# Mask and maximum matmuls on half the rows each, with new orders of work, in a two-layer decoder kernel

## The reference

```
x += window_attention(norm(x))          # layer 0: 16 heads, 7 neighbours, weights times a learned profile
x += masked_attention(norm(x), ctx)     # q = norm(x), k = v = ctx, 16 heads of 16; keys where mask == 0 get -1e9
x += slot_mixer(norm(x))                # top 8 of 64 slots, softmax, one GRU step, back by the same weights
x += causal_attention(norm(x))          # layer 1: causal, bias by position
x += cross_attention(norm(x), ctx)      # k, v from ctx, no mask
x += quantized_mlp(norm(x))             # ternary weights, hidden 1024, 3-tap conv, silu
```

## Time and profile before

| | us |
|---|---|
| median of 3 runs (3355.11 to 3357.54) | 3356.95 |
| the profiled execution | 3370.52 |
| its span, first to last instruction | 3368.7 |

### The profile page before, as it was taken

How to read it: one execution, slowest core, us unless ns; L and a number is a source line. 1 busy time by engine, 2 the same in 40 slices (tenths; PEclk the granted TensorE clock), 3 DMA queues, 4 the chain that set the end, 5 groups by cost and what they waited for, 6 DMA issues and landing times.

```text
span 3368.7 us, 61751 instructions
## 1 busy us (share of the span) xinstructions
PE 2962.4 (88%) x23406; PEld 2084.8 (62%) x23406; DVE 2265.4 (67%) x6662; ACT 2286.4 (68%) x5005; POOL 730.6 (22%) x1360
## 2 busy tenths in 40 slices
PE   4798978999889999899988999889998999989985
PEld 3566755666656666566665666556665666656663
DVE  6744499546885469854787548864589546985476
ACT  2358764788657786577765787657865778657783
POOL 1420023310332012320133102321032301232000
PEclk8899998999999999999999999999999999999997
DMA  4000000000000000000000000000000000000000
GB/s 153 1 1 1 1 26 12 9 1 4 23 20 1 1 15 12 20 1 1 15 23 9 1 4 15 20 9 1 4 23 20 1 1 15 12 20 1 1 5 10
DMA packets 43483, 43.59 MB, mean 13 GB/s; under 512 B 8577, under 2 KB 41185, under 8 KB 43185
## 3 DMA queue, kind: packets, MB, share of 16 engines
q1 hardware_dynamic: 41200, 36.46, 3.7%
q10 hardware_dynamic: 1984, 3.18, 0.3%
HBM read 31.24 MB, written 8.39 MB: 12 GB/s over the span
## 4 chain that ended last, share of the span: by engine, by line
PE 55%; DVE 20%; ACT 18%; issue 3%; POOL 2%; DMA 1%; SPq 0%; DVEq 0%; ACTq 0%; POOLq 0%
PE banks L1186 10%; PE banks L1219 9%; PE banks L1265 6%; PE banks L1228 4%; PE banks L1327 3%; ACT chain_arena L1025 3%; DVE chain_m L704 3%; PE banks L1261 3%; PE banks L1204 3%; ACT chain_arena L1046 2%; DVE chain_arena L898 2%; PE banks L1291 2%; ACT chain_xn L973 2%; DVE chain_arena L738 2%; PE banks L1411 2%
## 5 line engine op out<-in xcount | busy, mean ns | idle before, releaser
L1219 PE MATMUL banks<-chain_arena 64*128 64x256 f32 x3072 | 441.3, 410 | 18.3 <-DVE chain_m L704 15.5
L704 DVE TENSOR_REDUCE chain_m<-banks 128x4 f32<-128x512 f32 x512 | 330.7, 684 | 164.7 <-PE banks L1219 163.7
L1046 ACT ACTIVATE chain_arena<-chain_arena,chain_m 128x128 f32<-128x128 f32 x1024 | 322.9, 393 | 76.1 <-DVE chain_m L697 75.5
L1219 PEld LDWEIGHTS banks<-chain_arena 64*128 64x128 f32 x3072 | 278.6, 192 | 146.5 <-issue 84.7
L697 DVE CUSTOM_DVE_ANT_0 chain_arena<-banks,pos_bias 128x128 f32<-128x128 f32 x1024 | 226.5, 286 | 142.5 <-PE banks L1219 141.9
L1525 POOL TENSOR_SCALAR chain_rv<-chain_sq 128x2 f32<-128x2 f32 x160 | 35.2, 220 | 1263.8 <-ACT chain_xn L973 1262.0
L1265 PE MATMUL banks<-chain_arena 64*128 64x256 f32 x2048 | 293.0, 405 | 0.0
L1265 PEld LDWEIGHTS banks<-chain_arena 64*128 64x128 f32 x2048 | 177.4, 187 | 120.7 <-issue 109.0
L980 ACT ACTIVATE chain_xn<-chain_xa,chain_nm,chain_rs 128x256 f32<-128x256 f32 x384 | 207.5, 593 | 64.3 <-POOL chain_nm L1529 64.0
L671 DVE CUSTOM_DVE_ANT_0 chain_xa<-banks,chain_xa 128x256 f32<-128x256 f32 x320 | 122.4, 420 | 181.2 <-PE banks L1327 171.4
L1579 POOL TENSOR_TENSOR chain_arena<-chain_arena 128x512 f32<-128x512 f32 x128 | 165.4, 1304 | 279.7 <-DVE chain_arena L782 279.1
(11 more groups left out here) (315 smaller groups left out, 6894.9 us busy)
## 6 DMA issues: line engine op xcount, KB each, us to landing
chain_xn<-in_ctx SPq DMA_DIRECT2D x32, 256.0 KB, 2.8
chain_xa<-in_x SPq DMA_DIRECT2D x32, 256.0 KB, 3.1
out<-chain_xa SPq DMA_DIRECT2D x32, 256.0 KB, 2.2
chain_arena<-in_mask SPq DMA_DIRECT2D x32, 128.0 KB, 3.7
f_w1t<-in_w1t ACTq DMA_DIRECT2D x1, 1024.0 KB, 7.1
f_w2t<-in_w2t ACTq DMA_DIRECT2D x1, 1024.0 KB, 14.4
wqkv0T<-in_wqkv0T ACTq DMA_DIRECT2D x1, 768.0 KB, 16.8
whh<-in_whh SPq DMA_DIRECT2D x1, 768.0 KB, 10.0
```

The source lines that it names most:

```text
L704: e.tensor_reduce(m, s.rearrange("p (j o) t -> p j o t", o=2), AX.X, ALU.max, negate=True).then_inc(*done(f"{tag}_mx{u}"))
L1046: ex = e.activation(s, s, ACT.Exp, scale=-1.0, bias=max_of(t["m"], u // GROUPS, row_group(u), a))
L1219: mm[i] = e.matmul(c.ps[:, i, 2 * T * j:2 * T * j + 2 * T], t["qh"][p, j, x, b, :], flat(t["kx"][p, j, b]), start=not masked, stop=not mas ...
```

## The change

Three things. The key mask's matmul is split by rows as the scores are: for bank i it reads rows 64 i to 64 i + 63 of `first` and of the mask, and `first` has a row of ones at row 0 and at row 64. The matmul that spreads the maxima does the same with `pick` and mT; the three rows it needs lie in its half already. And all five lists of ORDER are replaced by others of the same length, with each chain as often in them as before. What is computed stays the same.

```diff
     if masked:
         for i in range(2):
-            e.matmul(c.ps[:, i, :], k["first"][:], spread(t["mask_bf"][:, T * b:T * b + T], 1, PER), start=True, stop=False)
+            p = slice(64 * i, 64 * i + 64)
+            e.matmul(c.ps[:, i, :], k["first"][p], spread(t["mask_bf"][p, T * b:T * b + T], 1, PER), start=True, stop=False)
...
         for i in range(2):
-            e.matmul(ps[:, i, :], k["pick"][:, 2 * i + o, :], flat(t["mT"][:, b]), start=True, stop=False)
+            p = slice(64 * i, 64 * i + 64)
+            e.matmul(ps[:, i, :], k["pick"][p, 2 * i + o, :], flat(t["mT"][p, b]), start=True, stop=False)
...
-        "rows_of": np.stack([(p // 32 == i) & (p % 32 < 3) for i in range(GROUPS)] + [p == 0], 1).astype(f),
+        "rows_of": np.stack([(p // 32 == i) & (p % 32 < 3) for i in range(GROUPS)] + [p % 64 == 0], 1).astype(f),
```

The lists, cut to the first and the last line of three of them:

```diff
     "sync": (
-        "0011223301031232001133220011332200113322001133220011332200113322"),
+        "0011223313123020131320201133220011332200113322001133220011332200"),
     "pool": (
-        "0132001133220132000101331313021232201232013201320132010310031123300201101122000033301111031101332203"
+        "1320113322001321011133311232202300321020302103210320131321133021112201333111310011333133223221300022"
...
-        "31122233330331232222123202302100213113233222"),
+        "22232322022002201200001003201132033022022000"),
     "tensor": (
-        "0132001030120110301331212020030233200210011311331133133301222322022210321301320130132012032132010210"
+        "1320113121310313123221011303211012021130330313323322102200212230010231001332130312103213120123103132"
...
-        "2031021033203203121221301321320312003013021233213232121123132123210301322302032112113121232323233323"
-        "23123123121223233333222222223222232332222222222"),
+        "1003203203203323203231023012322112020302323320320302202020020202032030220033002202202020202020020220"
+        "20202200202020020220202202200000022220000000000"),
```

More of the change, by code:

```diff
@@ L105 @@
-        "2233330331232222123202302100213110030020000331110201022331113110311222333303312322221232023021002131"
-        "1003002000033111020102233111311031122233330331232222123202302100213110030020000331110201022331113110"
-        "31122233330331232222123202302100213113233222"),
-    "vector": (
[L109 to L134, removed]
@@ L135 @@
-    "scalar": (
[L136 to L151, removed]
-        "1223231232122121120122212101023101310130123203203232023331330313133023031123102321231222020201302202"
-        "0202323302212032101032103030211030212102102100310301303100012100202001303102301300130130310001302103"
-        "1231032113201301101310113213021032121231211323112131120133023102331302031201302313302320210132332320"
-        "0320332103230032102320210213012313021223231232122121120122212101023101310130123203203232023331330313"
-        "1330230311231023212312220202013022020202323302212032101032103030211030212102102100310301303100012100"
-        "2020013031023013001301303100013021031231032113201301101310113213021032121231211323112131120133023102"
-        "3313020312013023133023202101323323200320332103230032102320210213012313021223231232122121120122212101"
-        "0231013101301232032032320233313303131330230311231023212312220202013022020202323302212032101032103030"
-        "2110302121021021003103013031000121002020013031023013001301303100013021031231032113201301101310113213"
-        "0210321212312113231121311201330231023313020312013023133023202101323323200320332103230032102320210213"
-        "0123130212232312321221211212211221313213113231232322323333333232332323232222222222222222"),
@@ new lines @@
+        "1320113322001321011133311232202300321020302103210320131321133021112201333111310011333133223221300022"
+        "2232021200003002012103113033211110231313111013221333003331322212300220222203200001001203112033311011"
+        "2111133312130133332233013001222323220220022012000010032011320331111011112133132310333322330130012223"
+        "2322022002201200001003201132033111101111213313231033332233013001222323220220022012000010032011320331"
+        "1110111121331323103333223301300122232322022002201200001003201132033111101111213313231033332233013001"
```

112 lines of the change are left out of this document (82 added, 30 removed).

## The result

The changed kernel takes 3328.49 us (median of 4 runs, 3322.95 to 3330.27), beside 3357.24 us for the kernel before on the same chip (3355.11 to 3359.25). The ratio is 0.9912, 95% interval 0.9894 to 0.9929: 0.9% faster, 29 us (24 to 36). The forecast was 3278 us, 79 us less than before. So the sign was right and the time lies in the range, but the gain is little over a third of the forecast. The profiled execution took 3329.9 us, its span 3328.1.

A forecast was written before the change was run, and what follows sets the result against it. TensorE was taken to set the pace, though not alone. From the profiled 3370.5 us: - 89 (edit) + 1 (ScalarE) + 10 (tail) = 3292.5, less 13.6 to the median: 3279, forecast as 3278 us; 8-of-10 range 3205 to 3332.

The forecast's parts named there:

- Step (1): Masked score groups on TensorE: half-row pairs start together, group 1.60 to 1.18 us, saving 141 us of TensorE, low end 46.
- Rival B: The two matmuls of a pair don't overlap: only 46 to 61 us of TensorE saved, 3334 us; chance 0.16.
- Step (2): Share of TensorE's saving that reaches the end time: 0.63 x 141 = 89 us, bounds 29 and 156.
- Rival A: The whole saving arrives, with the idle share of a turn unchanged: 156 - 10 us, 3211 us; chance 0.23.
- Step (3): Cost of the new lists: start 0 us, ScalarE's table loads 1, tail 10, middle 0.
- The end: Tail of the new lists: 35 more two-chain steps, taken at 10 us, bounds 0 and 19.
- The middle: Wider spacing of the chains' turns in the new lists: taken as 0 us, bounded above by 11 us of idle per turn.
- Rival C: Slower: new lists idle TensorE more than 55 us per turn, put at 3385 us; chance 0.05.
- Start and table loads: Start of the lists: 0 us, bounds -1 and +3; ScalarE's table loads 62 to 64, taken at 1 us.

The follow-up runs named there:

- x2: The kernel before with only the new lists, its matmuls still on full rows; ratio 1.018 to the kernel before, +60 us.
- x1: The changed kernel with the old lists, so both row-half edits alone; ratio 0.982 to the kernel before, -60 us.
- y2: Both row-half edits with the old lists reworked in two rounds, single steps moved over their whole length; ratio 0.9669 to the kernel before, 3253.65 us.
- x4: As x1, with a second half-row pair adding zeros behind each pair, 83 us more streaming; ratio 0.984 to the kernel before.
- x3: As x1, but the key mask's matmul on full rows again, so 256 of 384 groups are short; ratio 0.9849 to the kernel before.
- x6: The changed kernel with its new lists plus a second pair adding zeros behind each pair, 83 us of streaming; ratio 1.002 to the kernel before.
- x5: The changed kernel with single steps moved by a few places in the last 14% of each new list; ratio 0.986 to the kernel before.

## Why the prediction was right or wrong, by its steps

Idle and lower-clock time of the kernels, from their traces (us; turns are means of four steady ones, of three for x2 and the kernel after, whose first of the four is not yet a full turn):

| kernel | turn | TensorE busy | idle | last chain's end less the mean of the four | clock | time at 1.2 GHz |
|---|---|---|---|---|---|---|
| before | 400.5 | 362.9 | 37.5 | 54 | 0.965 | 236 |
| x1, edit | 393.5 | 348.4 | 45.1 | 56 | 0.961 | 258 |
| x2, lists | 406.0 | 369.4 | 36.6 | 84 | 0.951 | 336 |
| after, both | 392.5 | 352.8 | 39.7 | 83 | 0.943 | 379 |
| y2 | 388.1 | 345.9 | 42.3 | 53 | 0.968 | 208 |

**Step (1), the group: right.** 1.60 us became 1.18; the two matmuls of a pair start 3 ns apart and cost 0.22 us, and the busy time of the two lines fell to 151.9 us, just above the 120 to 150 forecast. Rival B is out. With the old lists TensorE lost 128 of the 141 us, with a clock that fell from 0.965 to 0.961. The rule of the Trainium skill, page "TensorE: Matmul & The Clock Gate", section "Measured speedup vs the span model", by which I had put the pair at an estimated 0.28 us, is not borne out for two matmuls of 64 rows: measured 0.22. The changed kernel shows only 89 us less, since it spends 379 us at the lower level in place of 236: 143 us more at half speed account for up to 72 us of busy time.

**Step (2), the share of 0.63: near in the new lists, too large in the old, and not a constant.** x1 turned 128 us into 60, a share of 0.47. The path from x4 shows how: the kernel before to x4 is 79 us less of TensorE and 54 us of time, 0.69 of it; x4 to x1 is 49 less and 7 of time, 0.14. Under the old lists the turn stops at 393 to 395 us, with two thirds of the groups short (x3) or with the pairs twice (x4) as with all. Two things do that. Waits: TensorE's idle part grows from 37.5 us per turn to 43.8 in x3 and 45.1 in x1. And the clock: x3 and x4 spend 31 and 34 us of four steady turns at 1.2 GHz, x1 89, so what x1 has less to stream it partly loses again. The forecast said that shorter TensorE work leaves more of its own time to waits, and then took one share for all of it, and nothing for the clock; with old lists that overstated the edit by 29 us. With the new lists (x2 to the kernel after) its worth is 90 us for 125 of TensorE, a share of 0.72. That this comes so near the forecast's 89 us is in part luck, since both factors are off: 125 for 141 us and 0.72 for 0.63. Rival A, the whole saving, is out: no comparison gave more than 90 of the 156 us.

**Step (3), the lists: the step that failed.** They were taken at 10 us, 0 to 19, all of it in the tail, and 0 for the middle. They cost 31 us with the edit (21 to 31 by the three measures above) and 60 without it. The miss is 50 us. Counted with the edit first it is 29 us of step (2) and 21 of this one; with the lists first all 50 are this one's. The two counts differ because the worth of each depends on the other; the lists are wrong in both, the share of step (2) in one. Where their cost lies, by TensorE's steps (2944 in each list), from the starts of the steps in the four traces:

| part | with the edit (x1 to after) | without it (before to x2) |
|---|---|---|
| before TensorE's first step | +2.4 | +2.8 |
| first 2833 steps | +4.9 | +30.9 |
| last 111 steps, to the end of the span | +18.4 | +24.6 |
| sum, the difference of the spans | +25.6 | +58.4 |

- *The end.* In the old lists the first chain ends 67 steps before the last, in the new ones 111. The last 111 steps took 162.3 us in x1 and 180.7 in the kernel after. This part of the forecast was sound in its working: the two-chain part has 58 steps in 93.0 us, 1.60 each (1.62 forecast), and 35 more such steps at 1.60 - 1.09 are 18 us, its upper bound of 19. What failed is the 10 that was taken out of the 0 to 19: the hope that one chain in causal attention and one in cross attention would fill each other better. TensorE was busy 67.30 of the 93.00 us, at a clock of 0.86, and a step took as long as in the old pair.
- *The middle.* I had put nothing here, since the trace could not price it, with up to 11 us of idle time per turn as a bound. With the edit the middle costs only 5 us, but not because nothing changed: over these steps (with 42 more of some 22400 matmuls among them) TensorE idled 28 us less and was busy 33 us more, with 304 us at 1.2 GHz in place of 204. Without the edit it idled 5 us more and was busy 25 us more, with 261 us in place of 198. By place, with the edit and without it: +19 and +17 us in the first 1104 steps, -6 and +21 in the next 1472, four steady turns, -8 and -7 in the rest. The turns show the same: idle time did not grow (36.6 and 39.7 us per turn, where the old lists have 37.5 and 45.1), busy time did, 362.9 to 369.4 and 348.4 to 352.8, for the same work. A steady turn of the kernel after (392.5 us) is no longer than one of x1 (393.5); that of x2 is 5.5 us longer than before. Rival C, "TensorE idle more than 55 us", looked for the lists' cost in the one place where it was not.

Over the whole span the clock covers the rise in busy time: TensorE's busy time at the 1.2 GHz level grew from 201 to 298 us with the edit and from 181 to 257 without it. Half of that, 49 and 38 us, is what half speed adds, and busy time rose by 39 and 36.

Start and table loads came out within their bounds. GpSimd's wait for the masks of a chain, now its second chain and not the third, ends at 76.08 us (start us, us, in brackets the wait; 77.16 in the earlier trace rows):

```profile
76.08 0.22 POOL L1558 TENSOR_SCALAR chain_mask_k<-chain_mask_c 128x2 f32<-128x2 f32 x1 [3.60 <-DMA chain_mask_c<-in_mask_cols]
```

ScalarE loads tables 64 times (32 at L1105, 20 at L1108, 12 elsewhere).

**Why the clock is lower with the new lists** can be seen, if not priced. In the kernel after, the waits of one steady turn (us, times, longest) have one that grew, while TensorE's idle time as a whole did not:

```profile
PE banks L1293 <- ACT chain_arena L1046: 13.1, 16, 2.4
```

In x1 it is 5.7 us in 8 waits and in the kernel before 4.0 (there L1291): causal attention's transposes wait for the exponentials. I read it as the chains standing so that fewer others can fill in. The idle time is also less evenly spread: over 1472 steps of steady turns TensorE has 60 waits of more than 1 us with the new lists, 86 us in all in the kernel after and 85 in x2, but 39 with 69 us in x1 and 36 with 60 us in the kernel before. Around one fall of the clock in the kernel after, two stretches next to each other, and two rows of TensorE's timeline there:

```profile
1802.50:1805.90 3.40, 1.42 (x10) 0.92 (x8) 3.40 (x19) 1.88 (x6) 0.00 (x0) 0.95 0.00 0
1805.90:1809.30 3.40, 2.00 (x18) 1.58 (x22) 3.33 (x7) 2.42 (x7) 0.00 (x0) 0.50 0.03 5
...
1805.07 0.73 PE L1293 MATMUL banks<-ident,chain_arena 128*128 128x128 f32 x4 [1.88 <-ACT chain_arena L1046]
1807.05 1.11 PE L1293 MATMUL banks<-ident,chain_arena 128*128 128x128 f32 x4 [1.25 <-ACT chain_arena L1046]
```

TensorE was busy 1.42 of 3.40 us, VectorE the whole time; in the next 3.40 us the clock is 0.50, the 1.2 GHz level. The two waits there are of the kind that grew. That the longer waits are what lowers the clock, and that the rise in busy time is the clock's, is inferred from busy times and clock, not shown by a run: none held the clock up with nothing else changed. x4 and x6 come nearest, and both add work. Open too is how much of x5's gain is its changed end.

## What to carry to other kernels

Where every engine follows a fixed order over interleaved chains, an edit and new lists are two changes: price and time them apart, each with the other held fixed, since neither the edit's worth (60 or 90 us) nor the lists' cost (31 or 60) is one number. Count where the last chain ends against the mean of all, and charge a wider end at the measured rate of one step with few chains left. The share of the critical chain is a fair first guess of what a microsecond is worth, but only until the waits of the old order and a falling clock take up what is saved; after that the order has to be made anew for the new durations, and compared with the old order kept. And look at busy time and clock of the same work as well as at idle time: here TensorE idled no more per turn under the new lists, and the same work took it longer.

## What the runs showed of the hardware

- Two bf16 matmuls of 64 rows and 512 columns, on the two halves of the rows and into two banks, start 3 ns apart and hold TensorE 0.22 us together, as one of 128 rows does in the kernel before (0.22 us between the two starts of a pair).
- The same work takes about twice as long at the lower level: the eight f32 matmuls behind a pair 1.84 us at 1.2 GHz, 0.96 at 2.4.
- Useless streaming can be nearly free: 83 us of it, next to matmuls of the same form, cost 7 us of time under the old lists (0 to 14 by the intervals), as the granted clock rose from 0.961 to 0.970; with 249 us it was 0.977. Under the new lists the same 83 us cost 36, at 0.954 in place of 0.943.
- The order of the same instructions alone moved the mean clock from 0.965 to 0.951, and TensorE's busy time from 2962.4 to 2998.5 us. Over all executions the clock was 0.962 to 0.971 with the old order and 0.949 to 0.953 with the new one.
